# Sums over the states of a selective scan: four halves at a time, each in a column group of TensorE, in place of two

## The chip, the cores and the metric

One core of one Trainium2 chip. The metric is the device time of one execution in microseconds (us). Before the change it is 3253.51 us, the median of three runs (3250.42 to 3253.9).

## The reference

Four layers, each on a layernorm of x and added to it, for 16 sequences of 512 tokens with 256 features, all in f32. The first is a selective scan (16 states for each feature), the second and the fourth are feed-forward layers whose operands are rounded to a four-bit format, the third is a linear attention. The change touches the scan alone:

```python
def step(h, inp):
    dtt, ut, bt, ct = inp
    dA = dtt[:, :, None] * A
    barA = jnp.exp(dA)
    inp_term = jnp.einsum('bdn,bn,bd->bn', dA, bt, ut)
    h = barA * h + inp_term[:, None, :]
    y = jnp.einsum('bdn,bn->bd', h, ct) + Dp * ut
    return (h, y)
...
x = x + _L0_attn_a_ref(_layernorm(x, axis=-1), ...)
x = x + _L0_ffn_ref(_layernorm(x, axis=-1), ...)
x = x + _L0_attn_b_ref(_layernorm(x, axis=-1), ...)
x = x + _L0_ffn_ref(_layernorm(x, axis=-1), ...)
```

## The kernel before, in words

The 16 sequences (`NB`, called batches) go through the kernel as a software pipeline. One body of the program is 32 beats long (`BEATS`), and several batches are in it at a time, each in another part: P (layernorm, the projections and dt), M and G (the scan), S and Y (the skip term and turning y back), R1 (first feed-forward layer and attention), R2 (second feed-forward layer). Bodies 0 to `LOOP_FROM` - 1 and the last ones are unrolled, those between run in a loop with two bodies to a round.

What sets the order is a schedule written out by hand. `PARTS_AT` (line 40) gives each part its first beat, the distance of its repetitions and their number; `TIMES` (line 43) gives each step of a part an offset on each engine. `start_of` adds them, and `order_of` sorts the steps by beat within a body. So each engine has one fixed order of steps; when a step really runs is decided by semaphores. A wait at the head of an engine holds back all that stands behind it there. The beats have no clock: a body lasts as long as its slowest chain.

The scan of one batch has 32 **halves** m = 0 to 31, one at each beat (part M). A half is a tile of 128 partitions by 512 tokens: 8 features of one row group times 16 states (`rows_of`). Two halves make one **state** n of the code (n = 0 to 15, m = 2n + h; this n counts pairs of halves). The way of a half:

- `spread_dt` on SP (lines 461 to 481): a DMA copies 8 rows of dt to 128 partitions of `scan_bufs`, 256 KB of writes. `scan_bufs` has four slots of two halves, so state n uses slot n % 4. Before state n + 4 may be spread, SP waits until the sum of state n is done (semaphore `summed`, lines 469 and 472). SP also issues the loads of x (`load`, line 457) and the stores of the result (`store`, line 490), all in one order, and waits at each.
- `decay` on ACT (lines 637 and 639): Exp and Square in place.
- `scan` on DVE (line 1210) and `read_state` on DVE (line 1220): the recurrence over the tokens, then the product with C.
- `sum_state` on PE (line 886): a matmul with a selection matrix `sel_y` (128 rows, 32 columns) that adds up the 16 states of each feature. Its result goes to 32 partitions of the PSUM bank `acc_y`. Which 32 is given by j of `rows_of`, which for halves in a row goes 0, 1, 2, 3, 0, ...; `tile_position=(0, 32 * j)` puts the matmul into column group j of the array.

After n = 7 and after n = 15 the skip term (`skip_term`, DVE, line 1225) reads `acc_y`; `turn_y` and `finish_y` then bring y back and add x, which frees the buffer of x for `load`. An f32 matmul stands in the trace as two records of MATMUL.

PE has the sum of n at beat 32 + 2n + 2.85, SP the spread of n at 32 + 2n - 1.75, ACT the decay of half m at 32 + m - 1.05, and DVE its scan and read at 32 + m - 0.03 and 32 + m + 0.6. The attention sums (line 1003) are matmuls of 32 columns in four column groups as well, with 128 tokens each.

Of the kernel before, what the change touches and what calls it, by code (L numbers as in the profile page):

```python
# [13 lines left out]
P = 128  # L14
NB, T, D = 16, 512, 256
TILES = T // P
DH = D // P
NS, RANK = 16, 64
# [16 lines left out]
HALVES = NS * DH  # L35
# [1 line left out]

PARTS_AT = {"P": (0, 0, 1), "M": (32, 1, 32), "G": (32, 2, 16), "S": (48.75, 16, 2), "Y": (65, 1, 2), "R1": (66, 3, 4), "R2": (95.7, 7, 4)}  # L40


TIMES = {
    "sp": {
        ("P", "load"): 2.8, ("G", "spread"): -1.75, ("R2", "down"): 12.8,
    },
# [49 lines left out]
def start_of(engine, part, step, t):  # L96

    first, gap, _ = PARTS_AT[part]
    return round(first + gap * t + TIMES[engine][part, step], 6)


def order_of(engine):

    steps = []
    for part, step in TIMES[engine]:
        for t in range(PARTS_AT[part][2]):
            k, beat = divmod(start_of(engine, part, step, t), BEATS)
# [72 lines left out]
def linear(batch, per, plus):  # L180

    if isinstance(batch, int):
        return batch * per + plus
    return batch.reg * (2 * per) + (batch.plus * per + plus)
# [29 lines left out]
def upto(batch, per, nth, inc=1):  # L214

    return linear(batch, per * inc, (nth + 1) * inc)


def rows_of(m):


    h, i = divmod(m, NS)
    return h, 4 * (i % 4) + i // 4


def build(nc, x_d, w_in_d, w_x_d, w_dt_d, b_dt_d, alog_d, dp_d, wa_d, ba_d, wp_d, bp_d, wg_d, wu_d, wd_d, out_d):
    ctx = ExitStack()
    with ctx:
# [6 lines left out]
        def sem(name):  # L235
            return ctx.enter_context(nc.semaphore(name))
# [129 lines left out]
        read_out, summed, c_ready = sem("read_out"), sem("summed"), sem("c_ready")  # L366
# [23 lines left out]
        def first(b, t=0):  # L390

            return isinstance(b, int) and b == 0 and t <= 0
# [11 lines left out]
        def batches(i, par, steps):  # L404

            for k, part, t, step in steps:
                if not isinstance(i, int) or 0 <= i - k < NB:
                    yield i - k, (par - k) % 2, part, t, step
# [380 lines left out]
        def _(pe):  # L789
            pe.wait_ge(s_set[0], N_SETUP_POOL)  # L790
            pe.wait_ge(s_set[2], 1)
            def turn_weights(which):

                raw, rows, width = raws[which]
                count = which * FTILES
                pe.wait_ge(s_set[2], 3 + which)
                if which < 2:
                    view = raw[0:rows, :].rearrange("p (a k) -> p a k", k=D)
                    for a in range(FTILES):
                        if count >= 2:  # L800
                            pe.wait_ge(s_set[1], count - 1)
                        for k in range(DH):
                            last = nc.tensor.transpose((acc_y, c_rep)[count % 2][:, k * FROWS:(k + 1) * FROWS],
                                                       view[:, a, k * P:(k + 1) * P], ident[0:rows, 0:rows])
                        last.then_inc(s_set[3], 1)
                        count += 1
                else:
                    view = raw[:, :].rearrange("p (a k) -> p a k", k=F)
                    for h in range(DH):
                        for k in range(FK):  # L810
                            cols = min(P, F - k * P)
                            pe.wait_ge(s_set[1], count - 1)
                            nc.tensor.transpose((acc_y, c_rep)[count % 2][0:cols, 0:P], view[:, h, k * P:k * P + cols],
                                                ident[:, :]).then_inc(s_set[3], 1)
                            count += 1
                    pe.wait_ge(s_set[1], count)
                    pe.wait_ge(s_set[2], 6)
# [49 lines left out]
            def project_c(b, par):  # L867

                wait_drained(pe, "P", b, 0, "u1")
                if not first(b):  # L870
                    pe.wait_ge(read_out, upto(b - 1, HALVES, HALVES - 1))
                for k in range(DH):
                    last = nc.tensor.matmul(c_rep[:, :], w_xC[:, k, :], u[par][:, k, :],
                                            start=(k == 0), stop=(k == DH - 1))
                last.then_inc(c_ready, 1)

            def sum_state(b, n):

                pe.wait_ge(read_out, upto(b, HALVES, DH * n + DH - 1))
                if n == NS // DH:  # L880
                    pe.wait_ge(skip_ready, upto(b, DH, 0))
                elif n == 0 and not first(b):
                    pe.wait_ge(skip_ready, upto(b - 1, DH, 1))
                for h in range(DH):
                    j, q = divmod(rows_of(DH * n + h)[1], 4)
                    last = nc.tensor.matmul(acc_y[32 * j:32 * j + 32, :], sel_y[:, q, :], bar[n % SLOTS][:, h, :],  # L886
                                            start=(q == 0), stop=(q == 3), tile_position=(0, 32 * j),
                                            skip_group_check=True)
                last.then_inc(summed, 1)

            def turn_y(b, par, j):

                pe.wait_ge(skip_ready, upto(b, DH, 1))
                to, done = take("Y", b, j, "y")
                for c in range(2):
                    for h in range(DH):
                        at = c * D + h * P
                        last = nc.tensor.transpose(to[:, at:at + P],
                                                   u[par][:, h, (2 * j + c) * P:(2 * j + c + 1) * P], ident[:, :])
                last.then_inc(done, 1)  # L900
# [133 lines left out]
            def run(i, par):  # L1034
                for b, q, part, t, step in batches(i, par, ORDER["pe"]):
                    if step == "C":
                        project_c(b, q)
                    elif part == "P":
                        part_p(b, q, step)
                        if first(b) and step == "dt1":  # L1040
                            turn_weights(0)
                            turn_weights(1)
                        elif first(b) and step == "G":
                            turn_weights(2)
                    elif part == "G":
                        sum_state(b, t)
                    elif part == "Y":
                        turn_y(b, q, t)
                    elif step.startswith("a_"):
                        attention(b, t, step)  # L1050
                    else:
                        ffn(f1 if part == "R1" else f2, b, t, step)
            bodies(pe, run)


# [326 lines left out]
```

## Time and profile before

| what | value |
|---|---|
| median of three runs | 3253.51 us |
| the profiled execution | 3258.51 us |
| its span, from the first to the last instruction | 3256.8 us |
| mean granted TensorE clock | 0.884 |
| PE, DVE, ACT, POOL busy | 78%, 76%, 58%, 35% of the span |
| DMA | 158 MB, mean 49 GB/s |

The durations in this document come from the profiled execution. The span is cut into the instructions of five engines and the DMA queue. Busy time leaves out waiting; for a matmul the ends are modelled. A row of the timeline merges instructions of one line that follow each other: start, duration, engine, line, result and operands, count, and in brackets how long the engine was idle before and who released it. PEclk 1.00 is a granted clock of 2.4 GHz, 0.5 one of 1.2 GHz. One body takes some 190 us.

### The profile page before, as it was taken

To read this page: it belongs to the slowest core of one execution; us is meant where nothing else is said; L and a number is where in the kernel's file an instruction comes from. 1 tells how busy PE (TensorE), PEld (TensorE's weight loads), DVE (VectorE), ACT (ScalarE), POOL (GpSimd) and SP (SyncE) were. 2 spreads that over 40 slices of the span, in tenths; PEclk is the share of its full clock that TensorE was granted. 3 is DMA by queue.
4 is the path that set the end of the run, shared out by engine and by line. 5 is a ranking of instruction groups with operands and counts; after the bars stand their busy time and mean duration, and the time that the engine had idled before them with its cause. 6 is when DMAs were issued, how large, how long until landed. Compare 5 with 4: busy or idle time off the path is not lost.

```text
span 3256.8 us, 44290 instructions
## 1 busy us (share of the span) xinstructions
PE 2547.0 (78%) x12844; PEld 1449.3 (45%) x12908; DVE 2482.7 (76%) x4197; ACT 1884.0 (58%) x3613; POOL 1127.5 (35%) x1601
## 2 busy tenths in 40 slices
PE   3438788797879888797978879697887979787875
PEld 1104445353535445363544535354453535445553
DVE  6468787978778797878879797788868788776642
ACT  3356657574755657475655748466574746644331
POOL 2003243433434343333334333343333334333331
PEclk8569799898989899898989989899988989888896
DMA  2344433434343333434333343334334343331000
GB/s 61 68 72 60 53 50 46 62 42 66 38 60 49 51 53 46 63 40 64 44 50 51 46 66 39 60 44 54 52 42 66 39 65 43 53 43 26 4 4 7
DMA packets 95654, 157.96 MB, mean 49 GB/s; under 512 B 10722, under 2 KB 29358, under 8 KB 95406
## 3 DMA queue, kind: packets, MB, share of 16 engines
q1 hardware_dynamic: 95406, 154.96, 34.3%
q8 instruction: 118, 1.93, 0.2%
q14 instruction: 130, 1.06, 0.1%
HBM read 12.33 MB, written 8.39 MB: 6 GB/s over the span
## 4 chain that ended last, share of the span: by engine, by line
PE 32%; DVE 21%; ACT 18%; issue 10%; DMA 8%; SPq 6%; POOL 5%; DVEq 0%; ACTq 0%; POOLq 0%
DMA scan_bufs<-dt 7%; PE bank L938 6%; PE bank L921 6%; SPq L480 6%; DVE scan_bufs L1210 4%; ACT p_xT L647 4%; DVE rounding L1077 3%; PE bank L978 2%; PE acc_y L886 2%; PE bank L959 2%; PE bank L918 2%; POOL f_h L565 2%; ACT scan_bufs L637 2%; ACT masked_scores L688 2%; DVE f_h_max L1104 2%
## 5 line engine op out<-in xcount | busy, mean ns | idle before, releaser
L1210 DVE TENSOR_TENSOR_SCAN scan_bufs<-scan_bufs,inp 128x512 f32<-128x512 f32 x512 | 714.0, 1394 | 66.5 <-ACT scan_bufs L639 56.7
L637 ACT ACTIVATE scan_bufs<-scan_bufs,a_rows 128x512 f32<-128x512 f32 x512 | 366.4, 716 | 345.8 <-DMA scan_bufs<-dt 343.9
L921 PE MATMUL bank<-w_gu,f_xqT 128*128 128x512 f32 x1024 | 509.3, 643 | 30.2 <-ACT f_xqT L688 28.5
L886 PE MATMUL acc_y<-scan_bufs,sel_y 128*32 128x512 f32 x1024 | 308.8, 685 | 225.7 <-DVE scan_bufs L1220 225.2
L938 PE MATMUL bank<-w_dn,f_hqT 128*128 128x256 f32 (+1 forms) x1536 | 425.8, 424 | 34.1 <-issue 24.8
L565 POOL TENSOR_TENSOR f_h<-f_h,f_h_inv 128x704 f32<-128x704 f32 x128 | 222.9, 1742 | 484.4 <-DVE f_h_inv L1108 484.4
L938 PEld LDWEIGHTS bank<-w_dn,f_hqT 128*128 128x128 f32 (+1 forms) x1536 | 301.4, 209 | 172.8 <-issue 131.5
L1220 DVE TENSOR_TENSOR scan_bufs<-scan_bufs,c_bank 128x512 f32<-128x512 f32 x512 | 338.2, 661 | 8.1 <-DVE x L1238 1.7
L583 POOL TENSOR_SCALAR_AFFINE_SELECT masked_scores<-masked_scores 128x512 f32<-128x512 f32 x256 | 190.2, 767 | 436.1 <-ACT masked_scores L688 436.1
L639 ACT ACTIVATE scan_bufs<-scan_bufs 128x512 f32<-128x512 f32 x512 | 322.6, 630 | 16.2
L565 POOL TENSOR_TENSOR f_h<-f_h,f_h_scale 128x704 f32<-128x704 f32 x128 | 195.7, 1529 | 388.8 <-DVE f_h L1079 388.8
L921 PEld LDWEIGHTS bank<-w_gu,f_xqT 128*128 128x128 f32 x1024 | 202.0, 205 | 281.9 <-issue 251.8
L931 PE MATMUL bank<-ident,f_h 128*128 128x128 f32 (+1 forms) x768 | 124.8, 304 | 149.2 <-POOL f_h L565 148.6
L724 ACT ACTIVATE f_tanh<-bank 128x512 f32<-128x512 f32 (+1 forms) x256 | 116.9, 457 | 179.2 <-PE bank L921 114.9
L1238 DVE TENSOR_TENSOR x<-bank,x 128x256 f32<-128x256 f32 x192 | 79.2, 412 | 176.3 <-PE bank L938 151.1
L886 PEld LDWEIGHTS acc_y<-scan_bufs,sel_y 128*32 128x32 f32 x1024 | 38.9, 113 | 374.0 <-DVE scan_bufs L1220 294.3
L918 PE MATMUL bank<-w_gu,f_xqT 128*128 128x384 f32 x512 | 205.0, 526 | 0.0
L712 ACT ACTIVATE f_h_abs<-f_h 128x704 bf16<-128x704 f32 x128 | 101.4, 792 | 149.4 <-POOL f_h L565 149.0
L931 PEld LDWEIGHTS bank<-ident,f_h 128*128 128x128 f32 (+1 forms) x768 | 88.2, 147 | 212.4 <-POOL f_h L565 171.2
L978 PE MATMUL bank<-q_par,fqk 32*128 32x128 f32 x2048 | 159.2, 297 | 29.7 <-ACT q_par L755 29.6
L688 ACT ACTIVATE masked_scores<-bank 128x512 f32<-128x512 f32 x256 | 137.8, 591 | 64.2 <-PE bank L978 63.9
L978 PEld LDWEIGHTS bank<-q_par,fqk 32*128 32x128 f32 x2048 | 133.6, 198 | 79.6 <-issue 41.4
(192 smaller groups left out, 4710.4 us busy)
## 6 DMA issues: line engine op xcount, KB each, us to landing
scan_bufs<-dt SPq DMA_DIRECT2D x512, 256.0 KB
xp<-L_attn_a_x SPq DMA_DIRECT2D x16, 512.0 KB, 7.6
out<-x SPq DMA_DIRECT2D x64, 128.0 KB, 1.7
w_attn<-L_attn_b_W_attn SPq DMA_DIRECT2D x1, 768.0 KB
scan_bufs<-L_ffn_w_gate SPq DMA_DIRECT2D x1, 704.0 KB
scan_bufs<-L_ffn_w_up SPq DMA_DIRECT2D x1, 704.0 KB
masked_scores<-L_ffn_w_down SPq DMA_DIRECT2D x1, 704.0 KB
w_in<-L_attn_a_w_in SPq DMA_DIRECT2D x1, 256.0 KB, 2.8
```

What stands on the lines that cost most here:

```text
L565: pool.tensor_tensor(d, s, spread(scale, width), ALU.mult).then_inc(signal, 1)
L637: nc.scalar.activation(half, half, ACT.Exp, scale=a_rows[:, c, at:at + 1]).then_inc(root_ready, 1)
L639: nc.scalar.activation(half, half, ACT.Square).then_inc(bar_ready, 1)
L688: nc.scalar.activation(dst, src[:, 0:width], ACT.Copy).then_inc(done, 1)
L886: last = nc.tensor.matmul(acc_y[32 * j:32 * j + 32, :], sel_y[:, q, :], bar[n % SLOTS][:, h, :], start=(q == 0), stop=(q == 3), tile_posit ...
L918: last = nc.tensor.matmul(to[:, 0:2 * (hi - lo)], f.xqT[:, k, :], w_gu[:, k, :, lo:hi], start=(k == 0), stop=(k == DH - 1))
L921: last = nc.tensor.matmul(to[:, :], f.xqT[:, k, :], w_gu[:, k, g, lo:hi], start=(k == 0), stop=(k == DH - 1))
L931: last = nc.tensor.transpose(to[0:n, k * P:(k + 1) * P], f.h[r][:, lo:lo + n], ident[:, :])
L938: last = nc.tensor.matmul(to[:, 0:D], f.hqT[0:n, k, :], w_dn[0:n, k, :], start=(k == 0), stop=(k == FK - 1))
L978: last = nc.tensor.matmul(to[:, at:at + P], fqk[r][rows, 1, grp, :], q_par[r][rows, odd, grp, :], start=True, stop=True)
L1210: nc.vector.tensor_tensor_scan(half, half, inp[par][:, :], 0.0, ALU.mult, ALU.add)\
L1220: nc.vector.tensor_tensor(half, half, c_rep[:, :], ALU.mult).then_inc(read_out, 1)
```

## The change

The part G, which had one step for each of 16 states, is split. D (the spreads of SP) keeps beat 32, distance 2 and 16 steps. G (the sums of PE) has 8 steps at distance 4, with the offset 4.85 in place of 2.85. `sum_states(b, t)` waits until half 4t + 3 has been read and then issues the matmuls of the four halves 4t to 4t + 3, whose column groups are 0 to 3. `summed` still counts up once for each state, behind the second and behind the fourth half. The waits for the skip term go to the steps t = 0 and t = 4, which hold n = 0 and n = 8 as before. `read_out` has no new updates: `upto(b, HALVES // 4, t, 4)` is the count at half 4t + 3. Nothing else is touched.

```diff
--- before.py
+++ after.py
@@ -37,17 +37,17 @@
 
 
 
-PARTS_AT = {"P": (0, 0, 1), "M": (32, 1, 32), "G": (32, 2, 16), "S": (48.75, 16, 2), "Y": (65, 1, 2), "R1": (66, 3, 4), "R2": (95.7, 7, 4)}
+PARTS_AT = {"P": (0, 0, 1), "M": (32, 1, 32), "D": (32, 2, 16), "G": (32, 4, 8), "S": (48.75, 16, 2), "Y": (65, 1, 2), "R1": (66, 3, 4), "R2": (95.7, 7, 4)}
 
 
 TIMES = {
     "sp": {
-        ("P", "load"): 2.8, ("G", "spread"): -1.75, ("R2", "down"): 12.8,
+        ("P", "load"): 2.8, ("D", "spread"): -1.75, ("R2", "down"): 12.8,
     },
     "pe": {
         ("P", "xT0"): 7.25, ("P", "xT1"): 8.1, ("P", "u0"): 10.8, ("P", "u1"): 14.2, ("P", "low"): 15.25,
         ("P", "B"): 16.5, ("P", "C"): 32.25, ("P", "dt0"): 20.5, ("P", "dt1"): 23.7, ("P", "G"): 29.6,
-        ("G", "sum"): 2.85, ("Y", "turn"): 0.2, ("R1", "turn_x"): 4.8, ("R1", "up0"): 6.3, ("R1", "up1"): 7.3,
+        ("G", "sum"): 4.85, ("Y", "turn"): 0.2, ("R1", "turn_x"): 4.8, ("R1", "up0"): 6.3, ("R1", "up1"): 7.3,
         ("R1", "turn_h"): 10.3, ("R1", "down"): 11.4, ("R1", "a_turn"): 14.35, ("R1", "a_qkv"): 15.3,
         ("R1", "a_s0"): 16.2, ("R1", "a_s1"): 17.35, ("R1", "a_sum"): 18.1, ("R1", "a_flip"): 19.3,
         ("R1", "a_turn_y"): 20.1, ("R1", "a_proj"): 21.0, ("R2", "turn_x"): 5.3, ("R2", "up0"): 5.8,
@@ -874,19 +874,21 @@
                                             start=(k == 0), stop=(k == DH - 1))
                 last.then_inc(c_ready, 1)
 
-            def sum_state(b, n):
-
-                pe.wait_ge(read_out, upto(b, HALVES, DH * n + DH - 1))
-                if n == NS // DH:
+            def sum_states(b, t):
+
+                pe.wait_ge(read_out, upto(b, HALVES // 4, t, 4))
+                if t == 4:
                     pe.wait_ge(skip_ready, upto(b, DH, 0))
-                elif n == 0 and not first(b):
+                elif t == 0 and not first(b):
                     pe.wait_ge(skip_ready, upto(b - 1, DH, 1))
-                for h in range(DH):
-                    j, q = divmod(rows_of(DH * n + h)[1], 4)
+                for m in range(4 * t, 4 * t + 4):
+                    n, h = divmod(m, DH)
+                    j, q = divmod(rows_of(m)[1], 4)
                     last = nc.tensor.matmul(acc_y[32 * j:32 * j + 32, :], sel_y[:, q, :], bar[n % SLOTS][:, h, :],
                                             start=(q == 0), stop=(q == 3), tile_position=(0, 32 * j),
                                             skip_group_check=True)
-                last.then_inc(summed, 1)
+                    if h == DH - 1:
+                        last.then_inc(summed, 1)
 
             def turn_y(b, par, j):
 
@@ -1043,7 +1045,7 @@
                         elif first(b) and step == "G":
                             turn_weights(2)
                     elif part == "G":
-                        sum_state(b, t)
+                        sum_states(b, t)
                     elif part == "Y":
                         turn_y(b, q, t)
                     elif step.startswith("a_"):
```

## Rows read from the trace of the kernel before

**Rows 1.** The page: span, engines, and two of its groups (busy, mean ns, idle before).

```profile
span 3256.8 us, 44290 instructions
...
PE 2547.0 (78%) x12844; PEld 1449.3 (45%) x12908; DVE 2482.7 (76%) x4197; ACT 1884.0 (58%) x3613; POOL 1127.5 (35%) x1601
...
L637 ACT ACTIVATE scan_bufs<-scan_bufs,a_rows 128x512 f32<-128x512 f32 x512 | 366.4, 716 | 345.8 <-DMA scan_bufs<-dt 343.9
...
L886 PE MATMUL acc_y<-scan_bufs,sel_y 128*32 128x512 f32 x1024 | 308.8, 685 | 225.7 <-DVE scan_bufs L1220 225.2
```

**Rows 2.** Windows: length; busy us (x instructions) of PE, PEld, DVE, ACT, POOL; PEclk; DMA.

```profile
1500.00:1520.00 20.00, 12.30 (x36) 4.52 (x36) 17.04 (x38) 8.23 (x15) 6.83 (x12) 0.74 0.51 79
1520.00:1540.00 20.00, 12.63 (x36) 5.64 (x37) 18.59 (x35) 11.20 (x23) 9.16 (x11) 0.91 0.45 71
1580.00:1611.00 31.00, 30.95 (x197) 19.81 (x197) 23.31 (x40) 19.72 (x42) 10.62 (x16) 1.00 0.29 36
1611.00:1655.00 44.00, 38.88 (x280) 27.23 (x282) 30.48 (x52) 41.91 (x76) 13.67 (x24) 0.92 0.33 42
```

**Rows 3.** Timeline, SP's DMA queue: start, us, merged spread DMAs (x count).

```profile
90.13 130.28 SPq L480 DMA_DIRECT2D scan_bufs<-dt  x38
...
1494.50 1.37 SPq L480 DMA_DIRECT2D scan_bufs<-dt  x2
...
1502.54 36.72 SPq L480 DMA_DIRECT2D scan_bufs<-dt  x10
```

**Rows 4.** Timeline, ACT, decays at L637; idle before, and what ended it.

```profile
112.98 0.72 ACT L637 ACTIVATE scan_bufs<-scan_bufs,a_rows 128x512 f32<-128x512 f32 x1 [3.31 <-DMA scan_bufs<-dt]
...
384.13 0.72 ACT L637 ACTIVATE scan_bufs<-scan_bufs,a_rows 128x512 f32<-128x512 f32 x1 [3.01 <-DMA scan_bufs<-dt]
...
1494.39 0.70 ACT L637 ACTIVATE scan_bufs<-scan_bufs,a_rows 128x512 f32<-128x512 f32 x1
...
1501.85 0.72 ACT L637 ACTIVATE scan_bufs<-scan_bufs,a_rows 128x512 f32<-128x512 f32 x1 [4.24 <-DMA scan_bufs<-dt]
...
1565.51 0.71 ACT L637 ACTIVATE scan_bufs<-scan_bufs,a_rows 128x512 f32<-128x512 f32 x1
```

**Rows 5.** The chain that ended last: shares by line; pieces (start us, us).

```profile
by line: issue 9.8%; DMA scan_bufs<-dt 7.0%; PE bank L938 6.1%; PE bank L921 6.0%; SPq L480 5.5%; DVE scan_bufs L1210 4.4%; ACT p_xT L647 3.5%; DVE rounding L1077 2.7%; PE bank L978 2.4%; PE acc_y L886 2.4%; PE bank L959 2.3%; PE bank L918 
...
1515.95 16.45 DMA scan_bufs<-dt
...
1592.32 0.98 PE acc_y L886 x4
```

**Rows 6.** Timeline, PE; x counts records, two to an f32 matmul.

```profile
354.87 1.05 PE L886 MATMUL acc_y<-scan_bufs,sel_y 128*32 128x512 f32 x4
...
364.25 1.92 PE L886 MATMUL acc_y<-scan_bufs,sel_y 128*32 128x512 f32 x4
...
1469.50 1.05 PE L886 MATMUL acc_y<-scan_bufs,sel_y 128*32 128x512 f32 x4
...
1475.62 1.05 PE L886 MATMUL acc_y<-scan_bufs,sel_y 128*32 128x512 f32 x4
...
1487.42 1.05 PE L886 MATMUL acc_y<-scan_bufs,sel_y 128*32 128x512 f32 x4
...
1495.80 1.05 PE L886 MATMUL acc_y<-scan_bufs,sel_y 128*32 128x512 f32 x4
...
1506.53 1.92 PE L886 MATMUL acc_y<-scan_bufs,sel_y 128*32 128x512 f32 x4 [5.47 <-DVE scan_bufs L1220]
...
1520.34 3.67 PE L921 MATMUL bank<-w_gu,f_xqT 128*128 128x512 f32 x8 [1.54 <-ACT f_xqT L688]
...
1553.15 1.05 PE L886 MATMUL acc_y<-scan_bufs,sel_y 128*32 128x512 f32 x4
...
1601.69 1.08 PE L1003 MATMUL bank<-masked_scores,vv 128*32 128x128 f32 x32
...
1679.03 4.83 PE L938 MATMUL bank<-w_dn,f_hqT 128*128 128x256 f32 x12 [5.80 <-issue]
```

## The prediction

> **What bounds the kernel now.** Names first. One body is 32 beats. Its scan work is 32 halves, called m0 to m31 here; state n has m2n and m2n+1. A half costs a spread DMA, two activations on ACT (the decay), a scan and a read on DVE, and its part of a sum on PE.
>
> I began with the page: PE is busy for 78% of the span and DVE for 76%, and neither is a bound by itself [rows 1]. So I cut one body into stretches [rows 2]. From 1500 to 1540 PE works only 12.3 and 12.6 of 20 us, while DVE has 35.6 of 40. From 1580 to 1611 PE is busy without a gap. From 1611 to 1655 ACT is (41.9 of 44).
>
> Then the queue of SP [rows 3]. The spreads of m4 and m5 are issued at 1494.50. m6 follows at 1502.54, behind the load of x, and the ten spreads from there run unbroken for 36.7 us. ACT starts the decay of m4 at 1501.85, after 4.24 us of idleness, in the moment of its landing [rows 4], and the chain that ended last passes through the spread of m10, which lands at 1515.95 + 16.45 = 1532.40 [rows 5]. So from the issue of m4 to the landing of m10 there are 37.9 us of pure transfer: 7.35 us for the first, then about 5.1 us each. Over the run ACT waits 343.9 us for spreads [rows 1].
>
> Last, the sums on that chain. In this body five pairs lie on it, n = 7, 8 (the row shown), 9, 14 and 15, with 0.98 to 1.01 us each, and the same stand there in nearly every body of batches 4 to 14. Over the whole chain the sums have 2.4%, 78 us [rows 5].
>
> **The change, part by part.** *The sums (PE).* The odd sum stays at its place in PE's order: 4t + 4.85 is the old 2n + 2.85 for n = 2t + 1. The even sum leaves its place two beats earlier and runs with the odd one. What do four at a time cost? A pair, four matmul records, takes 1.05 us, while a full-width f32 matmul of 512 columns is two records, eight of which take 3.67 us (0.46 us a record) [rows 6]. Two groups therefore run beside each other. That four do is shown by the attention sums: 32 records of 128 columns in four groups take 1.08 us, 34 ns each, where the full-width rate gives 115 ns [rows 6]. I take 1.07 us for a quad (bounds: 1.05, a pair, and 2.1, two pairs in a row), nearest to the 34 ns row. That saves 0.98 us of PE's time per quad, and there are 128.
>
> The Trainium skill (TensorE: Matmul & The Clock Gate, section "Part 3: Packing small matmuls — row/col tiling") is more cautious: it has three column tiles of 512 columns at 2.38 times and four row tiles at 3.07 times. By 3.07 an estimate for the quad would be 4 x 0.92 / 3.07 = 1.2 us, and the sum would be some 5 us higher, 0.13 us for each quad left on the chain.
>
> *What of it is on the path.* Of the chain's five sums per body only the even ones vanish, n = 8 and 14. 2/5 of 78 us is 31 us; I take **30 us**. The others lie where PE waits anyway: before 1506.53 it has been idle for 5.47 us for a read by DVE [rows 6]. Lower bound 20, if ACT or DVE is the next late one 0.3 us behind PE; upper 34, since a few more even sums lie on the chain of the first and last batches. The skip terms (they wait for n = 7 and 15) and C's projection keep their places and cost nothing.
>
> *The slots (SP and DMA).* The even slot comes free with the odd one, and the spread of state n + 4 waits for it on SP, in order, ahead of all that is behind it: store, load of x, further spreads. In most places slack covers this, and I cost it at nothing. The tightest is m16: it would wait for n = 5 (sum at 1553.15) [rows 6], issue at 1554.4 and land 7.35 us later, near 1561.7; its decay is at 1565.51 [rows 4]. Without that cover a late spread lands on the path one for one. Two places have no cover:
>
> 1. m4 and m5. They are freed by n = 14 today (sum at 1487.42) and by n = 15 afterwards (1495.80, ending at 1496.85) [rows 6]. SP gets to them at 1494.50 [rows 3], so their issue moves to 1497.0, by 2.5 us, and they open the unbroken stream in which each decay waits for its landing.
> 2. m0 to m3. They are freed by n = 12 and 13, now at 1469.50 and 1475.62 [rows 6]. m0 and m1 move by 6.1 us, and four spreads go out at once. Such a burst can be read at the start: issued from 90.13 on [rows 3], the fourth has landed at 112.98 [rows 4], 22.9 us later. From 1476.9 that is 1499.7, where the decay of m3 is at 1494.39 now [rows 4]. ACT stands still for 5 us, but its next decay waits until 1501.85 anyway, and the sum that needs m3 is at 1506.53. What reaches the path is that m4 queues behind m3: 1499.7 + 5 = 1504.7 in place of 1501.8.
>
> So a steady body has m4 landing some 2.4 us later (2.5 by the first reason, 2.9 by the second, less what the two transfers overlap). Upper bound of the cost: 2.4 us passed on whole. Lower bound: the stream is now unbroken from m0, and long streams run faster. The 38 spreads of the start took 130.28 us, 3.43 us each [rows 3], against 5.1 here. But DVE has only 4.4 us of idleness between 1500 and 1540 [rows 2], and no more than this can be won: 2.4 - 4.4 = -2.0 us. I take 1.4, nearer the upper end: the gain in speed shows late in a stream, and in four bodies (the row with 5.80 us of idleness at 1679.03 [rows 6]) PE stalls ahead of n = 15, m3 has landed by then, and the stream starts afresh at m4. 13 bodies x 1.4 = **18 us**.
>
> *The first batches.* There the distances are wider. In batch 1 the sums of n = 12 and 13 are at 354.87 and 364.25 [rows 6], and with the lower clock of the second m0 of batch 2 is issued 10 us later. The decay of m4 of batch 2 waits for its spread already (3.01 us idle at 384.13 [rows 4]). Bounds 0 and 10; I take 8. For batch 1 I take 5 within the same bounds, and 3 for late slots inside batch 0, which runs on the queue alone [rows 3]. Sum **16 us**, bounds 0 and 24.
>
> *The clock.* Without the even sums PE's gaps grow by 1 us. The granted clock is 0.74 between 1500 and 1520 [rows 2], and the sum behind the gap of 5.47 us took 1.92 us in place of 1.05 [rows 6], which is the 1.2 GHz level. These places are off the path. I cost it at 0, up to 5.
>
> **Sum:** 3258.5 (the profiled execution; its span is 3256.8 [rows 1]) - 30 + 18 + 16 = 3262.5. That execution is 5.0 us above the median of 3253.5, so against the median the sum is **3257.5**, 4 us more. A measurement of this kernel can tell about 0.2% (6.5 us) from no change.
>
> **The rivals.**
> *A, faster: the queue forgives.* The unbroken stream from m0 makes up what m4 lost (a body costs 0 to -1) and the start costs 5. For: 3.43 us a spread in the long run. Against: DVE's few idle us, and the four bodies that start afresh. 3253.5 - 30 + 5, less 0 to 13: 3216 to 3229, and up to 3240 if the start costs 16.
> *B, slower: the slots of m4.* The 2.4 us pass on whole in each body (13 x 2.4 = 31) and the start costs 22: 3253.5 - 30 + 53 = 3276. It decides from where the landing of m10 is late by more than the 2 us that PE saves per body. For: the decays from m4 on start at their landings. Against: see A.
> *C, slower: the four groups don't overlap* but run as two pairs, and the change doesn't do what it says. No saving, the delays of the forecast: 3287. Against: the 34 ns row.
> *D, slower: clock.* Longer gaps cost it on the path too: 5 to 10 us above the forecast, 3265. The trace has the drop only where PE waits for DVE [rows 6]. The Trainium skill (same page, section "Part 1: The HAM clock gate") says that the idle state is the 1.2 GHz one; the row of 1.92 us agrees.
>
> **How the numbers follow.** Forecast 0.33 (its own range is 3247 to 3268), A 0.31, B 0.28, C 0.04, D 0.04. Faster by over 0.2%: A and a little of the forecast, 0.34. Within: most of the forecast, 0.26. Slower: B, C, D and the forecast's upper end, 0.40. The range of 3228 to 3280 leaves out C, the far end of B and the lower part of A.
>
> **What would show it.** 128 groups of eight records of about 1.07 us, L886 busy near 150 us instead of 308.8 [rows 1] (C: near 300). n = 8 and 14 gone from the chain, whose share of sums falls to some 1.4%. The spreads of m4 issued 0.2 us after the last quad of the body ahead. ACT's wait for spreads up from 343.9 to some 380 us (A: no higher), with new waits at m2 and m3. Middle bodies within 1 us of their old length (A: 2 us shorter), the first three together 16 us longer. The forecast is wrong if the chain leaves the spreads of m4 to m10, or if m16 to m31 begin to wait for landings: then the slack that I cost at nothing was none.

## The result, and the profile after

The changed kernel takes **3282.94 us** (median of four runs, 3277.41 to 3290.55) beside 3253.7 us of the kernel before (four runs, 3250.42 to 3255.12). The ratio is 1.0098 with a 95% interval of 1.0081 to 1.0116: slower, by 29 us at the medians. 3257.5 was predicted, within 3228 to 3280. The changed kernel is on the side that had a chance of 0.40, and 3 us beyond the range. Rival B came nearest, with 3276. All medians here leave out disturbed executions: two of the twelve of e7, at granted clocks of 0.646 and 0.712, took 3733 and 3489 us.

The page of the changed kernel, the rows that answer to [rows 1]:

```profile
span 3283.1 us, 44274 instructions
...
PE 2453.7 (75%) x12908; PEld 1458.8 (44%) x12908; DVE 2479.4 (76%) x4197; ACT 1880.7 (57%) x3613; POOL 1127.1 (34%) x1601
...
L637 ACT ACTIVATE scan_bufs<-scan_bufs,a_rows 128x512 f32<-128x512 f32 x512 | 366.6, 716 | 413.8 <-DMA scan_bufs<-dt 411.7
...
L887 PE MATMUL acc_y<-scan_bufs,sel_y 128*32 128x512 f32 x1024 | 168.5, 736 | 237.5 <-DVE scan_bufs L1222 237.4
```

The sums cost 168.5 us in place of 308.8, so the change does what it says. PE as a whole is only 93 us less busy (2547.0 to 2453.7), since other matmuls take longer (those of L921, L923 in the changed kernel, 534.1 us in place of 509.3), with more of PE's time at the lower clock (below). ACT's wait for spreads has grown by 68 us, from 343.9 to 411.7. The span is 26.3 us longer.

The timeline of PE, one body (it answers to [rows 6]):

```profile
1502.24 1.06 PE L887 MATMUL acc_y<-scan_bufs,sel_y 128*32 128x512 f32 x8
...
1522.77 1.07 PE L887 MATMUL acc_y<-scan_bufs,sel_y 128*32 128x512 f32 x8
1536.22 1.94 PE L887 MATMUL acc_y<-scan_bufs,sel_y 128*32 128x512 f32 x8 [10.39 <-DVE scan_bufs L1222]
```

Eight records in 1.06 us, where four took 1.05. The first row is n = 12 and 13 (t = 6), the second n = 14 and 15 (t = 7), the third t = 0 of the next batch, at the low clock and behind 10.39 us of waiting. Before, PE had the sum of n = 0 in between (at 1500.01), and waited 5.47 us ahead of n = 1.

The DMA queue of SP in the same body (it answers to [rows 3]):

```profile
1503.55 10.45 SPq L480 DMA_DIRECT2D scan_bufs<-dt  x4
1521.42 0.35 SPq L490 DMA_DIRECT2D out<-x  x1
1524.00 2.38 SPq L480 DMA_DIRECT2D scan_bufs<-dt  x2
1528.98 1.69 SPq L457 DMA_DIRECT2D xp<-L_attn_a_x  x1
1530.86 37.05 SPq L480 DMA_DIRECT2D scan_bufs<-dt  x10
```

m0 to m3 go out together, 0.25 us after the quad of n = 12 and 13 has ended. m4 and m5 go out at 1524.00, 0.16 us after the end of the last quad (1523.84); before, they went out 2.35 us ahead of the end of that sum. Both are as forecast.

The decays on ACT (they answer to [rows 4]):

```profile
1521.57 0.72 ACT L637 ACTIVATE scan_bufs<-scan_bufs,a_rows 128x512 f32<-128x512 f32 x1 [1.39 <-DMA scan_bufs<-dt]
1526.80 0.72 ACT L637 ACTIVATE scan_bufs<-scan_bufs,a_rows 128x512 f32<-128x512 f32 x1 [3.85 <-DMA scan_bufs<-dt]
1532.80 0.72 ACT L637 ACTIVATE scan_bufs<-scan_bufs,a_rows 128x512 f32<-128x512 f32 x1 [4.31 <-DMA scan_bufs<-dt]
...
1561.63 0.72 ACT L637 ACTIVATE scan_bufs<-scan_bufs,a_rows 128x512 f32<-128x512 f32 x1 [2.56 <-DMA scan_bufs<-dt]
```

These are m2, m3, m4 and m10. m2 and m3 wait now, as forecast, and m4 starts 8.96 us after the end of the last sum of the batch ahead; before it was 1501.85 - 1496.85 = 5.00 us. So m4 is 4.0 us late in this body. m10 lands 37.8 us after that end in place of 35.55.

What stands behind the decay of m4 in ACT's fixed order is late with it: `f_x`, the normalised input of a feed-forward layer, and DVE waits for that. ACT's row and DVE's, after:

```profile
1534.09 0.58 ACT L693 ACTIVATE f_x<-x,f_below,f_rstd 128x256 f32<-128x256 f32 x1
...
1534.70 0.42 DVE L1106 TENSOR_REDUCE f_x_max<-f_x 128x16 f32<-128x256 f32 x1 [2.85 <-ACT f_x L693]
```

and DVE's before:

```profile
1505.01 0.42 DVE L1104 TENSOR_REDUCE f_x_max<-f_x 128x16 f32<-128x256 f32 x1 [0.19 <-DVE f_x L1079]
```

The chain that ended last (it answers to [rows 5]), its shares and four pieces of this body:

```profile
by line: DMA scan_bufs<-dt 12.8%; issue 9.2%; PE bank L940 6.4%; PE bank L923 5.9%; ACT p_xT L647 3.4%; PE bank L920 3.0%; DVE scan_bufs L1212 2.9%; DVE rounding L1079 2.8%; ACT scan_bufs L637 2.5%; PE acc_y L887 2.4%; SPq L480 2.4%; POOL f
...
1522.84 1.01 PE acc_y L887 x8
1524.00 8.78 DMA scan_bufs<-dt
...
1545.67 15.94 DMA scan_bufs<-dt
...
1585.55 1.00 PE acc_y L887 x8
```

Spreads have 12.8% of the chain, before 7.0%. In this body the chain now runs from the last quad (1522.84) straight into the spread of m4. From its landing it goes over ACT and DVE to the quad of t = 0 (1536.22), whose end frees the slot of m8 (issued at 1538.38), and through SP's spreads to that of m10, which lands at 1561.61: the link between sum, slot and spread is closed. The sums still have 2.4%, not the 1.4% of the forecast: n = 8 and 14 went as sums of their own, but the quad of t = 0 at the low clock (1.95 us here) has come onto the chain, and stands there in each of the 16 batches. The late slot of m8 was not priced; e9 and e10, which don't have it, cost as much as e11, which does.

Windows of the kernel after, from the end of the last sum to the landing of m10, and on to the end of the sum of n = 7 (length; busy us of PE, PEld, DVE, ACT, POOL; PEclk; DMA share):

```profile
1523.84:1561.63 37.79, 19.07 (x62) 8.19 (x62) 30.66 (x64) 15.35 (x29) 12.77 (x22) 0.77 0.48 75
1561.63:1609.20 47.57, 40.41 (x130) 21.03 (x130) 43.70 (x70) 24.60 (x51) 19.64 (x22) 0.89 0.34 47
```

The same stretches of the kernel before:

```profile
1496.85:1532.40 35.55, 20.04 (x63) 7.84 (x62) 31.46 (x64) 14.33 (x26) 13.35 (x22) 0.86 0.49 72
1532.40:1579.04 46.64, 41.30 (x130) 20.31 (x130) 44.12 (x69) 24.78 (x51) 20.02 (x22) 0.93 0.42 61
```

DVE's idle time in the first stretch grows from 4.1 to 7.1 us. The stretch is 2.2 us longer, and at its end DVE has done 0.8 us less. Of these 3 us of idle time, 2.7 are the wait ahead of `f_x_max` shown above (2.85 in place of 0.19). In the second stretch DVE has 44.1 of 46.6 us (before): no reserve there that would win this back.

Where the 26.3 us of the span are: the last sum of batch 0 ends 12.8 us later than before (228.16 against 215.39), that of batch 1 16.9 us (396.69 against 379.76), of batch 2 21.6 us (585.47 against 563.86), of batch 14 31.6 us (2845.80 against 2814.18). So the first three batches cost 21.6 us, the twelve from there 10.0, 0.8 us each, and the end gives 5.3 back. In batch 0, on PE, after:

```profile
160.83 1.06 PE L887 MATMUL acc_y<-scan_bufs,sel_y 128*32 128x512 f32 x8
168.36 1.94 PE L887 MATMUL acc_y<-scan_bufs,sel_y 128*32 128x512 f32 x8 [5.41 <-DVE scan_bufs L1222]
195.10 1.94 PE L887 MATMUL acc_y<-scan_bufs,sel_y 128*32 128x512 f32 x8 [10.70 <-DVE scan_bufs L1222]
```

and before:

```profile
150.55 1.05 PE L886 MATMUL acc_y<-scan_bufs,sel_y 128*32 128x512 f32 x4 [0.46 <-DVE scan_bufs L1220]
161.06 1.05 PE L886 MATMUL acc_y<-scan_bufs,sel_y 128*32 128x512 f32 x4
164.82 1.05 PE L886 MATMUL acc_y<-scan_bufs,sel_y 128*32 128x512 f32 x4 [2.71 <-DVE scan_bufs L1220]
```

The sum of n = 6 was at 150.55 and is in the quad at 160.83. It frees the slot of n = 10, that is of m20 and m21. Their decays on ACT, and that of m22, after:

```profile
169.65 0.72 ACT L637 ACTIVATE scan_bufs<-scan_bufs,a_rows 128x512 f32<-128x512 f32 x1 [3.91 <-DMA scan_bufs<-dt]
174.37 0.72 ACT L637 ACTIVATE scan_bufs<-scan_bufs,a_rows 128x512 f32<-128x512 f32 x1 [3.34 <-DMA scan_bufs<-dt]
179.74 0.72 ACT L637 ACTIVATE scan_bufs<-scan_bufs,a_rows 128x512 f32<-128x512 f32 x1 [3.98 <-DMA scan_bufs<-dt]
```

and before:

```profile
165.68 0.72 ACT L637 ACTIVATE scan_bufs<-scan_bufs,a_rows 128x512 f32<-128x512 f32 x1 [1.12 <-DMA scan_bufs<-dt]
167.62 0.72 ACT L637 ACTIVATE scan_bufs<-scan_bufs,a_rows 128x512 f32<-128x512 f32 x1 [0.56 <-DMA scan_bufs<-dt]
171.74 0.72 ACT L637 ACTIVATE scan_bufs<-scan_bufs,a_rows 128x512 f32<-128x512 f32 x1 [2.73 <-DMA scan_bufs<-dt]
```

4, 7 and 8 us late: SP issues m20 at 162.06 in place of 153.71, after the quad. Each of these decays waits for its landing, so a slot that comes free late starts the lag that ends as 12.8 us.

### The profile page after: what moved, and what is told of

It is laid out like the page before. It is cut to its first block, busy times and chain, and to the rows that moved or that the text cites. A ratio compares the mean times of both kernels' runs of the same rounds, so it can differ in the third digit from the quotient of the medians.

```text
span 3283.1 us, 44274 instructions
## 1 busy us (share of the span) xinstructions
PE 2453.7 (75%) x12908; PEld 1458.8 (44%) x12908; DVE 2479.4 (76%) x4197; ACT 1880.7 (57%) x3613; POOL 1127.1 (34%) x1601
## 3 DMA queue, kind: packets, MB, share of 16 engines
q14 instruction: 130, 1.06, 0.1%
## 4 chain that ended last, share of the span: by engine, by line
PE 32%; DVE 20%; ACT 18%; DMA 13%; issue 9%; POOL 5%; SPq 3%; DVEq 0%; ACTq 0%; POOLq 0%
DMA scan_bufs<-dt 13%; PE bank L940 6%; PE bank L923 6%; ACT p_xT L647 3%; PE bank L920 3%; DVE scan_bufs L1212 3%; DVE rounding L1079 3%; ACT scan_bufs L637 2%; PE acc_y L887 2%; SPq L480 2%; POOL f_h L565 2%; PE bank L961 2%; PE bank L980 2%; ACT masked_scores L688 2%; PE bank L933 2%
## 5 line engine op out<-in xcount | busy, mean ns | idle before, releaser
L637 ACT ACTIVATE scan_bufs<-scan_bufs,a_rows 128x512 f32<-128x512 f32 x512 | 366.6, 716 | 413.8 <-DMA scan_bufs<-dt 411.7
L923 PE MATMUL bank<-w_gu,f_xqT 128*128 128x512 f32 x1024 | 534.1, 670 | 51.8 <-ACT f_xqT L688 47.3
L923 PEld LDWEIGHTS bank<-w_gu,f_xqT 128*128 128x128 f32 x1024 | 213.9, 216 | 317.2 <-issue 272.9
L887 PE MATMUL acc_y<-scan_bufs,sel_y 128*32 128x512 f32 x1024 | 168.5, 736 | 237.5 <-DVE scan_bufs L1222 237.4
L920 PE MATMUL bank<-w_gu,f_xqT 128*128 128x384 f32 x512 | 211.9, 541 | 0.0
L887 PEld LDWEIGHTS acc_y<-scan_bufs,sel_y 128*32 128x32 f32 x1024 | 21.7, 117 | 304.4 <-DVE scan_bufs L1222 264.3
```

The lines of the kernel that those rows point to most:

```text
L637: nc.scalar.activation(half, half, ACT.Exp, scale=a_rows[:, c, at:at + 1]).then_inc(root_ready, 1)
L920: last = nc.tensor.matmul(to[:, 0:2 * (hi - lo)], f.xqT[:, k, :], w_gu[:, k, :, lo:hi], start=(k == 0), stop=(k == DH - 1))
L923: last = nc.tensor.matmul(to[:, :], f.xqT[:, k, :], w_gu[:, k, g, lo:hi], start=(k == 0), stop=(k == DH - 1))
```

## The experiments

The theory they test: the change is a saving of some 30 us on PE and a cost of some 60 us by slots that come free later, through SP. The rivals: the quads cost more than they seem to; the clock; only the start; only one of the two slots (m4's or m0's). The runs report medians and ratios; a number of us "by the ratio" is the ratio less 1, times that median before. All ratios are to the kernel before on the same chip, with 95% intervals; its medians there were 3252.87 us (e1 to e4), 3252.32 (e5 to e8) and 3248.94 (e9 to e12).

Most of the kernels rest on one edit: the part G is split into an even place E, the old place of the even sum, and the odd place G, and a function says which quads are joined. With `True` it is the change, with `False` the kernel before. The edits are shown shortened.

```diff
-"G": (32, 4, 8)                    ("G", "sum"): 4.85
+"E": (32, 4, 8), "G": (32, 4, 8)   ("E", "sum"): 2.85, ("G", "sum"): 4.85
+def sums(b, t, even):
+    if even and joined(b, t):
+        return
+    states = [2 * t] if even else [2 * t, 2 * t + 1] if joined(b, t) else [2 * t + 1]
+    ...
```

### Slots and sums taken apart

**e1_slots**: nothing is joined, but each spread waits for the sum that it would wait for with quads.

```diff
-sp.wait_ge(summed, upto(b, NS, k - SLOTS))
+sp.wait_ge(summed, upto(b, NS, (k - SLOTS) | 1))
-sp.wait_ge(summed, upto(b - 1, NS, k - SLOTS + NS))
+sp.wait_ge(summed, upto(b - 1, NS, (k - SLOTS + NS) | 1))
```

> Sums in pairs at their old places, but each spread waits until the odd sum of its two states is done, as if four were summed at a time. So it has the slots' delay and none of the saving on PE. If the slots are the cause: the first bodies as long as with the change (the last sum of batch 0 about 13 us later than before, batch 2's m10 about 20 us), the middle ones 2.5 to 3 us longer than before (1.2 us of queue and the two sums that the change saves are still there), total 3290 to 3300. If the slots are harmless and the lower clock behind the longer gaps is the cause: 3254, as before.

Measured: 3311.94 us, ratio 1.0191 (1.016 to 1.0223). The slots alone cost 62 us, and the change, which has the same waits and the joined sums, costs 32 (0.98%). So joining saves some 30 us. 3290 to 3300 had been expected; the late slots cost more. From e1's page:

```profile
L637 ACT ACTIVATE scan_bufs<-scan_bufs,a_rows 128x512 f32<-128x512 f32 x512 | 366.5, 716 | 397.9 <-DMA scan_bufs<-dt 395.7
...
L894 PE MATMUL acc_y<-scan_bufs,sel_y 128*32 128x512 f32 x1024 | 312.2, 692 | 256.1 <-DVE scan_bufs L1228 255.7
```

The sums cost what they cost before, and most of ACT's added wait is there all the same.

**e4_serial**: the change, but the second pair of each quad waits until the first has ended, so that only two groups run beside each other.

```diff
+if len(states) == 2 and n == states[1]:
+    pe.wait_ge(summed, upto(b, NS, states[0]))
```

> The change, but the second pair of each four waits until the first is done, so that they can't overlap. If four run at once now: about 1.1 us more for each of the three sums on the chain, 13 x 3.3 = 43 us, 3315 to 3330. If the four had run as two pairs all along: within 0.2% of 3283.

Measured: 3318.94 us, ratio 1.0222 (1.0198 to 1.0247), 36 us above the change at the medians (40 by the ratios). Its quads on PE, at the high and at the low clock:

```profile
1533.68 2.17 PE L896 MATMUL acc_y<-scan_bufs,sel_y 128*32 128x512 f32 x8
1549.39 3.91 PE L896 MATMUL acc_y<-scan_bufs,sel_y 128*32 128x512 f32 x8 [11.59 <-DVE scan_bufs L1230]
```

2.17 us serial, 1.06 with the overlap: the four groups run beside each other in full, and rival C is out.

**e5_six_pairs** and **e6_six_quads**: six slots in place of four, so that a slot is used again after five states, or more, in place of four; e5 with pairs, e6 with quads.

```diff
-SLOTS = 4
+SLOTS = 6
+SLOT_OF = (0, 1, 2, 3, 4, 0, 1, 2, 3, 4, 0, 1, 2, 3, 4, 5)
```

(and the waits on the last use of the slot instead of the fourth state back)

> The kernel before with six slots in scan_bufs in place of four, dealt so that a state comes back to its slot after 5 or 6 states and not after 4. Sums in pairs. A control for the next run. In the kernel before m4 is held by the place of the store in SP's order and m6 by the load of x, not by a slot, so little should change: 3245 to 3254. If slots hold up the kernel before as well: under 3240.

> The change with the same six slots: each spread may go out at least as early as with pairs and four slots. If late slots are the whole cost of the change, the saving on PE is left, 1.8 us a body and some more at the end, 25 to 30 us against the control: 3222 to 3232. If joining the sums costs something of its own (clock, the later start of the even one): 3245 to 3285, near or above the control.

Measured: e5 3248.72 us, ratio 1.0001 (0.9987 to 1.0014); e6 **3227.33 us**, ratio 0.9922 (0.9906 to 0.9938). Two more slots alone bring nothing that can be measured. With them the joined sums win 21 us at the medians, and 0.8% (26 us) by the ratios, over the same kernel with pairs. 25 to 30 had been expected, so a small price of the joining itself isn't excluded. The queue of SP in e6:

```profile
1489.58 1.36 SPq L484 DMA_DIRECT2D scan_bufs<-dt  x2
1496.54 0.40 SPq L461 DMA_DIRECT2D xp<-L_attn_a_x  x1
1497.19 38.74 SPq L484 DMA_DIRECT2D scan_bufs<-dt  x10
```

and the quad of t = 7 beside it on e6's PE:

```profile
1490.33 1.06 PE L898 MATMUL acc_y<-scan_bufs,sel_y 128*32 128x512 f32 x8
```

m4 is issued at 1489.58, 1.8 us before the last quad ends (1491.39), as with pairs. This kernel is faster than the one before and than the change.

### Which slots, and where

**e2_start**: the change, but with pairs in batches 0 and 1.

```diff
+def joined(b, t):
+    return not (isinstance(b, int) and b < 2)
```

> The change, but batches 0 and 1 are summed in pairs. If the start costs what the two traces show, the 21.6 us by which the third batch is late fall away: 3262, and the middle bodies keep their 0.8 us. If the lateness of the start would be made up later anyway: 3275 to 3283.

Measured: 3257.7 us, ratio 1.0019 (1.0004 to 1.0034). Without the joined sums of the first two batches 26 us of the 32 are gone (1.0098 to 1.0019). So the start carries most of the net loss, and the steady part nearly breaks even.

**e9 to e12** take the waits of e1 apart; all have pairs at the old places. e9_gate_m4 holds m4 and m5 back for n = 15 (k == 2), e10_gate_m0 holds m0 and m1 back for n = 13 (k == 0), both from batch 3 on. e11_gate_late has all late waits behind the start, e12_gate_start only those of the start.

```diff
-sp.wait_ge(summed, upto(b - 1, NS, k - SLOTS + NS))
+sp.wait_ge(summed, upto(b - 1, NS, (k - SLOTS + NS) | int(k == 2 and late)))   # e9
+sp.wait_ge(summed, upto(b - 1, NS, (k - SLOTS + NS) | int(k == 0 and late)))   # e10
+late = not (isinstance(b, int) and b < 3)
```

The bounds of e11 and e12 fit together: a late wait of e1 is in one of the two, and in one alone.

> The kernel before, sums in pairs. From batch 3 on only the spreads of m4 and m5 wait for n = 15 in place of n = 14 (13 batches). If the later issue of m4 is a cost by itself, 2.5 us of delay passed on whole: 3253 + 13 x 2.4 = 3284; passed on in part, because the stream catches up: 3262 to 3275; if only the burst from m0 costs: 3253.

> The kernel before, sums in pairs. From batch 3 on only the spreads of m0 and m1 wait for n = 13 in place of n = 12. m3 then lands behind the issue of m4 in the bodies without PE's stall. If queueing m4 behind m3 is a cost by itself: in some 9 of 13 bodies 2 to 3 us, 3253 + 18 to 27 = 3271 to 3280, and together with the run before not the sum of both but little more than the larger. If an unbroken stream makes up for it: 3253 to 3260.

> The kernel before, sums in pairs, with the late slots of the change in the batches after the start (spreads of batch 3 on, and the later ones of batch 2). The run with all slots late had bodies 2.5 us longer: 3253 + 32 = 3285. If that length came from what the start left behind: near 3253.

> The kernel before, sums in pairs, with the late slots of the change only in batches 0 and 1 and the first two states of batch 2. Two runs (the change with and without its start) differ by 25 us: 3253 + 20 to 26 = 3273 to 3279. Together with the run before it should make up the 58 us of the run with all slots late.

| kernel | median us | ratio | 95% interval | us of ratio |
|---|---|---|---|---|
| e9_gate_m4 | 3281.07 | 1.0093 | 1.0079 to 1.0107 | +30 |
| e10_gate_m0 | 3278.81 | 1.0086 | 1.0070 to 1.0102 | +28 |
| e11_gate_late | 3283.24 | 1.0096 | 1.0081 to 1.0111 | +31 |
| e12_gate_start | 3274.74 | 1.0073 | 1.0050 to 1.0097 | +24 |

Either slot alone costs as much as all of them together. In e9, SP's queue (m4 and m5, then m6 to m15) and ACT's decays of m3 to m5:

```profile
1511.10 1.37 SPq L480 DMA_DIRECT2D scan_bufs<-dt  x2
...
1516.82 36.22 SPq L480 DMA_DIRECT2D scan_bufs<-dt  x10
```

```profile
1508.45 0.71 ACT L637 ACTIVATE scan_bufs<-scan_bufs,a_rows 128x512 f32<-128x512 f32 x1
1518.44 0.72 ACT L637 ACTIVATE scan_bufs<-scan_bufs,a_rows 128x512 f32<-128x512 f32 x1 [6.78 <-DMA scan_bufs<-dt]
1523.78 0.72 ACT L637 ACTIVATE scan_bufs<-scan_bufs,a_rows 128x512 f32<-128x512 f32 x1 [3.46 <-DMA scan_bufs<-dt]
```

and the same of e10:

```profile
1508.28 4.91 SPq L480 DMA_DIRECT2D scan_bufs<-dt  x2
...
1517.87 32.40 SPq L480 DMA_DIRECT2D scan_bufs<-dt  x10
```

```profile
1513.65 0.72 ACT L637 ACTIVATE scan_bufs<-scan_bufs,a_rows 128x512 f32<-128x512 f32 x1 [3.86 <-DMA scan_bufs<-dt]
1519.26 0.72 ACT L637 ACTIVATE scan_bufs<-scan_bufs,a_rows 128x512 f32<-128x512 f32 x1 [3.92 <-DMA scan_bufs<-dt]
1524.18 0.72 ACT L637 ACTIVATE scan_bufs<-scan_bufs,a_rows 128x512 f32<-128x512 f32 x1 [3.06 <-DMA scan_bufs<-dt]
```

The last sum ends at 1510.91 in e9 and at 1510.63 in e10. m4 starts 7.5 us after it in e9, because it is issued late. In e10 it is issued early, at 1508.28, and starts 8.6 us after it all the same, because it shares the queue with m2 and m3. That is why the two don't add up: both work through the one landing of m4 and what stands behind its decay on ACT (the table below). The working in the prediction took them so ("less what the two transfers overlap"), and this part of it held.

e12's start (24 us) and e11's rest (31) make 55 us, where e1 has 62; their intervals cover the difference. The forecasts for e9 to e12 held within 2 us.

### What is left of the gain with four slots

**e7_join_t4** joins only n = 8 and 9, **e8_no_t67** leaves n = 12 to 15 and the first two batches in pairs.

```diff
+    return t == 4                                            # e7
+    return t < 6 and not (isinstance(b, int) and b < 2)      # e8
```

> Four slots. Only the sums of n = 8 and 9 are joined (step t = 4), all others stay in pairs at their old places. The slot of n = 8 is needed by m24 and m25, which wait for their decays by 18 us and more. If the gain of a joined sum on the chain is what the two traces show (0.8 us between n = 7 and 9) and nothing is late: 3253 - 13 x 0.8 = 3242. If late slots cost there too: 3253 or more.

> The change without its joined steps t = 6 and 7 (n = 12 to 15 in pairs, whose slots m0 to m7 need) and without any in batches 0 and 1. If only the slots of m0 to m5 and the start cost: the same as with n = 8 and 9 alone, 3242. If the slots of m8 to m31 cost in the middle too: above that by as much, up to 3257 (the run in which just batches 0 and 1 are in pairs).

Measured: e7 3236.03 us, ratio 0.9953 (0.9937 to 0.9968); e8 3238.67 us, ratio 0.9963 (0.995 to 0.9976). One joined quad of eight wins 15 to 16 us. That fits half of the 30, one of the two even sums that the chain had in each body; 11 had been expected. Joining t = 0 to 3 and 5 as well, as e8 does from batch 2 on, adds nothing that can be measured, as the forecast had it for sums that lie where PE waits anyway. Of the two, n = 14 can't be had with four slots, since it is the slot of m4.

### The clock

**e3_warm**: the change, and at the old places of n = 2, 4 and 6 two matmuls with weights of zero into the same bank, to keep PE busy. They add nothing to the result but zeros.

```diff
+if t in (1, 2, 3):
+    for j in range(2):
+        nc.tensor.matmul(acc_y[32 * j:32 * j + 32, :], zero_w[:, :],
+                         w_in[:, :, :].rearrange("p k e -> p (k e)"), start=False, stop=False,
+                         tile_position=(0, 32 * j), skip_group_check=True)
```

> The change, with two matmuls with zero weights (which add nothing) at the old places of n = 2, 4 and 6, where PE waits for DVE. If the longer gaps cost clock on the path between the landing of m10 and the sum of n = 7 (47.5 us against 46.1 before): that stretch is back at 46, the time at the lower clock in a body falls by some 9 us, total 3283 - 13 x 1.4 = 3265. If the stretch is longer for another reason (DVE behind the landings): 3280 to 3290, the clock up and the stretch the same.

Measured: 3277.53 us, ratio 1.0095 (1.0071 to 1.0118), against 1.0098 of the change: no difference that can be told.

The mean body of the batches 3 to 14, cut at the ends of sums and at the landing of m10 (the start of its decay), says the same (us; worked out from the traces, one profiled execution each):

| stretch | before | change | e1 | e3 | e4 | e6 | e7 | e8 | e9 | e10 | e11 |
|---|---|---|---|---|---|---|---|---|---|---|---|
| end of n = 15 to landing of m10 | 35.9 | 37.1 | 36.2 | 37.1 | 37.5 | 36.2 | 35.9 | 35.9 | 36.4 | 36.1 | 36.3 |
| landing of m10 to end of n = 7 | 46.0 | 47.5 | 47.8 | 47.6 | 49.8 | 46.1 | 46.2 | 46.3 | 47.3 | 47.6 | 47.8 |
| n = 7 to n = 15 | 105.6 | 103.8 | 106.0 | 103.2 | 103.5 | 103.8 | 104.6 | 104.8 | 106.4 | 106.4 | 105.9 |
| total | 187.5 | 188.4 | 190.1 | 187.9 | 190.8 | 186.1 | 186.6 | 187.1 | 190.0 | 190.1 | 190.0 |
| n = 15 to n = 7, PE at 1.2 GHz | 18.5 | 27.6 | 21.9 | 24.5 | 25.0 | 23.9 | 18.2 | 24.8 | 22.5 | 20.8 | 22.2 |
| n = 15 to n = 7, DVE idle | 7.1 | 9.8 | 9.3 | 9.3 | 10.9 | 7.6 | 7.1 | 7.6 | 9.0 | 8.9 | 9.3 |
| of it, ahead of the `f_x_max` behind m4 | 0.2 | 2.2 | 2.2 | 2.1 | 2.4 | 0.2 | 0.2 | 0.2 | 1.5 | 1.7 | 2.0 |

*The clock.* PE spends 9 us more of this part of a body at 1.2 GHz in the change. But e1 has 3.4 us more only, and 47.8 us from the landing of m10 to n = 7; e3 has 3 us less than the change, and the same 47.6. e8 has 6 us more than before and no late m4, and its stretch takes 46.3. So the longer stretches are the slots', not the clock's. A smaller effect of the clock remains possible: e3 took back only a third of the time at 1.2 GHz, and its interval is 8 us to either side.

*Where the late slots enter.* In every version with a late m4, DVE waits for ACT's `f_x`, which stands behind the decay of m4 in ACT's order; where m4 is in time, that wait is 0.2 us. In e9 it grows by 1.3 us, and the way from n = 15 to n = 7 by 1.7; in e11 by 1.8 and 2.1, in the change by 2.0 and 2.6.

## Why the prediction was wrong, step by step

**Right: the sums.** 1.07 us for a quad was taken, 1.06 to 1.07 measured. 30 us of saving was the term. e1 against the change gives 29 to 30, e5 against e6 gives 21 to 26, and e7's 15 fit the half of it that hangs on n = 8. One reading was wrong: in the bodies of batches 4 to 14 four sums stand on the chain, n = 8, 9, 14 and 15, and a fifth in batches 4, 8 (the body shown) and 14 alone. The sums of n = 8 and 14 make 28 us of the whole chain, so the term of 30 was near all the same. The estimate of 1.2 us, worked out from the 3.07 times of the Trainium skill (TensorE: Matmul & The Clock Gate, section "Part 3: Packing small matmuls — row/col tiling"), was too high: four matmuls of 0.92 us each [rows 6] in 1.06 us is 3.5 times. The place was right too: in the table the change is 2.2 us shorter than e1 from n = 7 to n = 15.

**Right in the steady bodies: the cover of m16 to m31.** m16 was to land near its decay, without harm. In this body it lands 2.6 us ahead of it, and the decays of m16 to m31 never wait for a spread in the steady bodies. e8, which has all the late slots inside a batch up to t = 5, isn't slower than e7 by more than the intervals hold. In batch 0 the sign of being wrong did come: m20 and m21 wait 3.9 and 3.3 us in place of 1.1 and 0.6, and m29 to m31, which never waited before, wait too. There the slack that was costed at nothing was none.

**Wrong in size: m4 in the steady bodies.** That m4 lands late and that this costs time was right. It lands 3.6 us late in the mean (2.4 to 4.8; 4.0 in the body shown), where 2.4 were forecast. What failed is the step "I take 1.4, nearer the upper end", by which 13 bodies cost 18 us: e11 measures 31, 2.4 a body, and the body of e9, where m4 is 2.5 us late, grows by 2.5 (190.0 - 187.5). The step let a faster stream win time back, up to the 4.4 us in which DVE stands idle between 1500 and 1540 [rows 2]. The stream did get faster: from the issue of m4 to the landing of m10 it takes 38.3 us before, 37.0 in the change and 36.2 in e9 (means of batches 3 to 14; 37.9 and 37.6 in the bodies shown), so in e9 m10 is only 0.5 us late. It did not help. DVE had lost its time by then, at `f_x_max` behind the decay of m4, and its later waits in the stream grew no shorter: its idle time from n = 15 to n = 7 rose from 7.1 to 9.0 us in e9 and to 9.8 in the change. Behind m10 DVE has 44.1 of 46.6 us, and nothing is won back there.

**Wrong in size: the start.** 16 us were forecast; e12 measures 24 (by its interval 16 to 32), and the trace of the change has 21.6 by the end of batch 2, with the joined sums in it. In e12's own trace batch 0 is 13.9 us late, batch 2 27.1, batch 14 20.7. The step that failed is "3 for late slots inside batch 0, which runs on the queue alone". Batch 0 lost 12.8 us. That it runs on the queue alone is just why a late slot counts there: nothing else hides it. Batches 1 and 2 lost 4.2 and 4.7 more, in place of 13. So those two were overestimated and batch 0 was missed.

**Wrong: two of the signs.** ACT's wait for spreads rose to 411.7, not to some 380. The share of the sums on the chain stayed at 2.4%, because of the quads of t = 0.

**The rivals.** A is refuted: its stream did win back up to 2 us by the landing of m10, but the body grew all the same (e9 to e11, 28 to 31 us). C is refuted by the rows of 1.06 and by e4. D's drop of the clock came (0.884 to 0.861 in the mean), its price did not. B's numbers, 31 for the bodies and 22 for the start, are those of e11 and e12 within their intervals. Its condition, a landing of m10 late by more than the 2 us that PE saves, held in the body shown (2.2 us) but not in the mean (1.2 us). So B's number is in part luck: its delay goes through ACT's order to DVE, and not through the landing of m10. The forecast was the middle between A and B, and no row stood for that middle. What stands behind the decay of m4 in ACT's order, and DVE's busy share behind m10, would have told that the delay passes on nearly whole.

**Open:** the wait at `f_x_max` was read from the traces; no kernel with `f_x` ahead of the decay of m4 was run. It leaves 0.1 to 0.6 us of the growth up to n = 7, and 0.3 to 0.8 us behind n = 7 (e1, e9 to e11), unexplained. Nor was it tried why the change gets 5.3 us back behind batch 14 (3.7 of them by the last sum of batch 15).

## What to carry to other kernels

Joining the work of a consumer also joins the release of its buffers: write down, for each buffer, who waits for its release and what stands behind that wait in the queue, and price it where the landings set the pace. There a late head of a stream cost four fifths of its delay or all of it here, though the stream caught up. The engine that waits for the transfer has a fixed order: look at what else stands behind that wait, and who needs it. Idle time of DVE elsewhere in the stream was no reserve. If the saving itself is real, as here, buy it with buffers (two more slots: 3227 us in place of 3283), or join only where the chain has the sum and no spread waits for the slot (3236).

## What was not expected of the hardware

- Two delays in one queue of transfers cost 0.93% and 0.86% alone, and with all the other late slots behind the start 0.96%. Both delay the same landing, and they don't add up.
- A fall of the mean granted clock from 0.884 to 0.861 cost nothing that could be told from the noise: e8, with 6.5 us more at 1.2 GHz in each body than e7, takes 3239 us beside 3236.
- The fastest kernel of all, e6, has a mean granted clock of 0.869, while e5, with 0.887, is 21 us slower. In this range the mean clock says little about the time.
